# Summing the key products of a Performer block by 32x32 blocks turned on VectorE, in place of products on TensorE

## The chip, the core and the metric

One core of one Trainium2 chip runs the whole kernel in one launch. The metric is the device time in microseconds (us) from the launch's start to its end. The engines are TensorE (PE, with its weight loads PEld), VectorE (DVE), ScalarE (ACT), GpSimd (POOL) and SyncE (SP), which here issues all transfers.

## What is computed

Rows are 8 batches of 1024, model width 512, 16 heads of 32, 128 random features. The part that the change touches is the linear attention's sum over the keys:

```python
pk  = phi(k * scale, omega)                     # 128 features per head
kv  = einsum('bhsm,bhsk->bhmk', pk, v)          # 128 x 32 for each head
z   = sum(pk, axis=2)                           # 128 for each head
num = einsum('bhsm,bhmk->bhsk', pq, kv)
den = einsum('bhsm,bhm->bhs', pq, z)
out = x + layernorm(x + attn) -> FFN -> layernorm, plus a gated block on shifted rows
```

## The kernel before

Three passes follow one another, each closed by a barrier of all engines: `keys_pass`, `attend_pass`, `feed_forward_pass`. Each walks 32 groups of 256 rows, four groups to a batch. fp32 products are made of three products of rounded parts (`product`, L97), so each operand is split in a hi part (ACT) and a lo part (DVE or POOL).

Each engine runs a list of jobs written out by hand, in order: `PE_BODY`, `DVE_BODY`, `ACT_BODY`, `POOL_BODY`, `SP_BODY`. An entry is (job, number, lead): in the body of group g it works on group g + lead. Engines meet in semaphores alone. No engine goes past a job whose wait isn't met.

In `keys_pass` the jobs of one body are these. `turn_x` transposes normalised rows (PE, hi on ACT, lo on DVE). `k`, `q`, `v` are products of 12 matmuls into one of three PSUM banks, `ring`. `turn_k` transposes the keys; `proj` (L652) makes the features in four banks `feat`; `top` (L565, four reductions on DVE, then `below` L569) finds the maxima; `exp` (ACT L512) makes `e`, `hi` (ACT L519) and `pk` (DVE L575) split it. `kv` (PE L676) multiplies the features of four heads by their values, 128 x 512, into a `ring` bank, from which DVE adds it to `kv_sum` (L584, L586). POOL adds the features over the rows in `z` (L457), and in `whole` (L442) puts xT together for a store. The banks bind the order: the second `k` product of a body waits until DVE has taken `kv` number 0 out of `ring[0]`, and `turn_x` number 1 waits for DVE's lo part of number 0.

What is in `kv_sum` is laid out by (32 values x 4 heads) on partitions and (4 heads x 128 features) on columns, so only the diagonal blocks are wanted, and with the features on the columns, while the next pass needs the features on partitions. The job `fold` does this for one quarter (four heads, number c) in each body after a batch has ended: for each head one matmul against the 0/1 matrix `fold` (L695), which turns and picks, and one of `z_all` against a column of ones `fold_z` (L696), both fp32, into the bank `turn`, which `turn_x` also uses. ACT copies 128 x 136 out of it to `kv_out` (L526), and after the fourth quarter SP stores `kv_out` to `kv_d` (L410). 28 bodies have one fold; the last has four, at the end of the pass.

In `attend_pass` one transfer for each batch loads `kv_in` (L856), in the pass's head for batch 0, and as the last SP job of a batch's first group for the next. ACT and DVE split it into `kvz` (L1062 to L1163). SP's list in a body begins with `load_x` and then carries the denominators out, back, inverted out and back (`den_store`, `den_load`, `rden_store`, `rep_load`), which DVE's `recip` (L1132) waits for.

Of the kernel before, what the change touches and what calls it, by code (L numbers as in the profile page):

```python
# [242 lines left out]
def keys_pass(nc, x, wq, wk, wv, omega, xn_d, xT_d, u_d, kv_d, n_batches, groups_per_batch):  # L243
# [11 lines left out]
    with ctx:  # L255
# [51 lines left out]
        fold_made, folded, fold_out = sem("fold_made"), sem("folded"), sem("fold_out")  # L307
# [32 lines left out]
        def fold_bank(g, c):  # L340
            return feat[c].t if g == G - 1 else turn

        def rows(j):
# [3 lines left out]
        PE_BODY = [("kv", 0, -1), ("proj", 0, 0), ("k", 0, 1), ("kv", 1, -1), ("k", 1, 1), ("kv", 2, -1), ("q", 0, 1),  # L347
                   ("proj", 1, 0), ("turn_k", 0, 1), ("kv", 3, -1), ("q", 1, 1), ("turn_k", 1, 1), ("v", 0, 1),
                   ("fold", 0, -1), ("turn_x", 0, 2), ("v", 1, 1), ("turn_x", 1, 2)]
        DVE_BODY = [("top", 0, 0), ("kv", 0, -1), ("kv", 1, -1), ("stats", 0, 2), ("kv", 2, -1), ("sq", 0, 1),  # L350
                    ("top", 1, 0), ("turn_k", 0, 1), ("pk", 0, 0), ("pk", 1, 0), ("pk", 2, 0), ("kv", 3, -1),
                    ("turn_k", 1, 1), ("sq", 1, 1), ("pk", 3, 0), ("pk", 4, 0), ("pk", 5, 0), ("turn_x", 0, 2),
                    ("v_out", 0, 1), ("pk", 6, 0), ("v_out", 1, 1), ("turn_x", 1, 2), ("pk", 7, 0)]
# [13 lines left out]
        def run(eng, do, order):  # L367
            def body(g, b, i):

                for job, n, lead in order:  # L370
# [3 lines left out]
                    if job == "fold" and not pieces(g + lead) or job == "sums" and NC - 1 not in pieces(g + lead):  # L374
                        continue
# [11 lines left out]
        def _(sp):  # L387
# [3 lines left out]
            def do(job, n, g, b, i):  # L391
# [1206 lines left out]
```

## Time and profile before

| | us |
|---|---|
| median of 3 runs | 3691.76 (3691.68 to 3693.3) |
| profiled execution, time | 3692.05 |
| its span, first to last instruction | 3690.2 |
| TensorE busy | 3544.2 (96%) |
| VectorE busy | 2070.7 (56%) |
| ScalarE busy | 1839.5 (50%) |
| GpSimd busy | 1394.2 (38%) |

The keys pass lasts until about 948 us of the span, the attend pass until about 2120, the rest is the feed-forward pass. Busy shares are means over all three; the rows further below are from single bodies. L12 is line 12 of the kernel.

### The profile page before, as it was taken

To read this page: it belongs to the slowest core of one execution; us is meant where nothing else is said; L and a number is where in the kernel's file an instruction comes from. 1 tells how busy PE (TensorE), PEld (TensorE's weight loads), DVE (VectorE), ACT (ScalarE), POOL (GpSimd) and SP (SyncE) were. 2 spreads that over 40 slices of the span, in tenths; PEclk is the share of its full clock that TensorE was granted. 3 is DMA by queue.
4 is the path that set the end of the run, shared out by engine and by line. 5 is a ranking of instruction groups with operands and counts; after the bars stand their busy time and mean duration, and the time that the engine had idled before them with its cause. 6 is when DMAs were issued, how large, how long until landed. Compare 5 with 4: busy or idle time off the path is not lost. (4 is left out here: it accounts for less than half of the span.)

```text
span 3690.2 us, 71667 instructions
## 1 busy us (share of the span) xinstructions
PE 3544.2 (96%) x27762; PEld 3105.4 (84%) x27762; DVE 2070.7 (56%) x3304; ACT 1839.5 (50%) x3976; POOL 1394.2 (38%) x957
## 2 busy tenths in 40 slices
PE   7999999999699999999999949999999999999998
PEld 6888888887588888888888849988889989888887
DVE  5877777777567777777777633333333333333332
ACT  5777777777456656565665633333333323333332
POOL 2554545454244545454454412222222222222222
PEclk9999999999799999999999979999999999999999
DMA  2222222221223232232323241111111111111111
GB/s 104 87 78 70 90 78 73 73 88 54 95 81 102 82 97 91 88 97 88 102 84 98 83 129 68 46 44 43 45 44 46 45 38 46 44 43 45 45 45 46
DMA packets 151680, 262.70 MB, mean 71 GB/s; under 512 B 23184, under 2 KB 44176, under 8 KB 151440
## 3 DMA queue, kind: packets, MB, share of 16 engines
q1 hardware_dynamic: 151440, 259.46, 20.9%
q8 instruction: 155, 2.54, 0.3%
q14 instruction: 85, 0.70, 0.1%
HBM read 155.48 MB, written 103.94 MB: 70 GB/s over the span
## 5 line engine op out<-in xcount | busy, mean ns | idle before, releaser
L1484 DVE TENSOR_TENSOR ffn_hT_lo<-ffn_hid,ffn_hT_hi 128x512 fp32r<-128x512 f32 x256 | 334.3, 1334 | 489.4 <-ACT ffn_hT_hi L1460 489.4
L97 PE MATMUL ffn_hidden<-ffn_yT_hi,ffn_wa_hi 128*128 128x256 f32 x2048 | 573.3, 280 | 11.8 <-DVE ffn_yT_lo L1480 11.8
L97 PE MATMUL ffn_hidden<-ffn_yT_hi,ffn_wa_lo 128*128 128x256 f32 x2048 | 573.3, 280 | 0.0
L97 PE MATMUL ffn_hidden<-ffn_yT_lo,ffn_wa_hi 128*128 128x256 f32 x2048 | 572.3, 279 | 0.0
L1451 ACT ACTIVATE ffn_hid<-ffn_hidden,ffn_bias 128x256 f32<-128x256 f32 x512 | 213.2, 467 | 669.6 <-PE ffn_hidden L97 650.8
L233 POOL TENSOR_TENSOR ffn_n_rstd<-ffn_n_base,ffn_n_power 128x2 f32<-128x2 f32 x32 | 22.4, 700 | 1073.7 <-DVE ffn_n_negmean L228 1073.7
L97 PE MATMUL ffn_result<-ffn_wb_hi,ffn_hT_hi 128*128 128x512 f32 x1024 | 412.2, 403 | 2.6 <-DVE ffn_hT_lo L1484 2.6
L97 PE MATMUL ffn_result<-ffn_wb_hi,ffn_hT_lo 128*128 128x512 f32 x1024 | 404.5, 395 | 0.0
L97 PE MATMUL ffn_result<-ffn_wb_lo,ffn_hT_hi 128*128 128x512 f32 x1024 | 404.2, 395 | 0.0
L97 PEld LDWEIGHTS ffn_hidden<-ffn_yT_hi,ffn_wa_hi 128*128 128x128 f32 x2048 | 384.5, 188 | 20.8 <-DVE ffn_yT_lo L1480 12.1
L97 PEld LDWEIGHTS ffn_hidden<-ffn_yT_lo,ffn_wa_hi 128*128 128x128 f32 x2048 | 385.0, 188 | 8.8
L97 PEld LDWEIGHTS ffn_hidden<-ffn_yT_hi,ffn_wa_lo 128*128 128x128 f32 x2048 | 385.2, 188 | 0.0
L457 POOL TENSOR_TENSOR keys_z_sum<-keys_z_sum,keys_e 128x512 f32<-128x512 f32 x192 | 265.2, 1402 | 307.3 <-ACT keys_e L512 307.3
L512 ACT ACTIVATE keys_e<-keys_feat,keys_below 128x128 f32<-128x128 f32 x1024 | 280.6, 420 | 22.8 <-DVE keys_below L569 22.7
L575 DVE SCALAR_TENSOR_TENSOR keys_pk_lo<-keys_e,keys_pk_hi 128x512 fp32r<-128x512 f32 x256 | 219.3, 887 | 25.7 <-ACT keys_pk_hi L519 25.5
L97 PEld LDWEIGHTS ffn_result<-ffn_wb_hi,ffn_hT_hi 128*128 128x128 f32 x1024 | 192.1, 188 | 48.4 <-DVE ffn_hT_lo L1484 10.2
L97 PEld LDWEIGHTS ffn_result<-ffn_wb_hi,ffn_hT_lo 128*128 128x128 f32 x1024 | 192.2, 188 | 46.9
L1107 DVE TENSOR_REDUCE attend_top<-attend_feat 128x4 f32<-128x512 f32 x256 | 159.0, 684 | 125.3 <-PE attend_feat L1200 125.3
L1126 DVE SCALAR_TENSOR_TENSOR attend_pT_lo<-attend_feat,attend_pT_hi 128x512 fp32r<-128x512 f32 x256 | 163.3, 683 | 116.7 <-ACT attend_pT_hi L988 116.3
L97 PEld LDWEIGHTS ffn_result<-ffn_wb_lo,ffn_hT_hi 128*128 128x128 f32 x1024 | 192.4, 188 | 38.0
L565 DVE TENSOR_REDUCE keys_top<-keys_feat 128x4 f32<-128x512 f32 x256 | 159.0, 684 | 107.7 <-PE keys_feat L652 107.7
L1464 ACT ACTIVATE ffn_s<-ffn_s,ffn_n_shift,ffn_n_rstd 128x512 f32<-128x512 f32 x64 | 48.7, 809 | 338.7 <-POOL ffn_n_shift L235 338.7
(238 smaller groups left out, 9876.8 us busy)
## 6 DMA issues: line engine op xcount, KB each, us to landing
attend_uq<-u_d SPq DMA_DIRECT2D x33, 512.0 KB, 4.6
ffn_y_in<-y_d SPq DMA_DIRECT2D x33, 512.0 KB, 3.6
keys_xin<-in_L_attn_x_dram SPq DMA_DIRECT2D x32, 512.0 KB, 5.3
xn_d<-keys_xn SPq DMA_DIRECT2D x32, 512.0 KB, 4.2
xT_d<-keys_xT_whole SPq DMA_DIRECT2D x32, 512.0 KB, 2.6
u_d<-keys_uq SPq DMA_DIRECT2D x32, 512.0 KB, 2.8
attend_xTf<-xT_d SPq DMA_DIRECT2D x32, 512.0 KB, 5.1
r_d<-attend_gate SPq DMA_DIRECT2D x32, 512.0 KB, 3.2
```

The costliest lines, as they stand in the source:

```text
L97: last = pe.matmul(out, stationary[a], moving[b], start=start and n == 0, stop=stop and n == len(TERMS) - 1)
L233: pool.tensor_tensor(self.rstd[:, :], self.base[:, :], self.power[:, :], ALU.pow).then_inc(self.root, 1)
L457: pool.tensor_tensor((z_all if last_of_batch else z_sum)[:, c, :], z_sum[:, c, :], e[t][:, c, :], ALU.add).then_inc(z_added[t], 1)
L512: last = act.activation(e[t][:, c, j * M:(j + 1) * M], feat[j].t[:, c * M:(c + 1) * M], ACT.Exp, bias=below[:, t, h:h + 1])
L565: dve.tensor_reduce(top[:, n, :, j:j + 1], feat[j].t[:, :].rearrange("p (c m) -> p c m", c=NC), AX.X, ALU.max).then_inc(top_ready, 1)
L575: dve.scalar_tensor_tensor(out=pk[t].lo[:, c, :], in0=e[t][:, c, :], scalar=FLOOR, in1=f32(pk[t].hi[:, c, :]), op0=ALU.add, op1=ALU.subtract)\
L1107: dve.tensor_reduce(top[:, n, :, j:j + 1], feat[j].t[:, :].rearrange("p (c m) -> p c m", c=NC), AX.X, ALU.max).then_inc(feat[j].free, 1)
L1126: dve.scalar_tensor_tensor(out=pT[j].lo[:, :], in0=feat[j].t[:, :], scalar=FLOOR, in1=f32(pT[j].hi[:, :]), op0=ALU.add, op1=ALU.subtract)\
L1451: last = act.activation(hid[n % 2][:, a, :], bank.t[:, a * GT:(a + 1) * GT], ACT.Gelu, bias=bias1[:, 2 * n + a:2 * n + a + 1])
L1464: act.activation(s[:, t, :], s[:, t, :], ACT.Identity, bias=norm.shift[:, t:t + 1], scale=norm.rstd[:, t:t + 1]).then_inc(normed, 1)
L1484: dve.tensor_tensor(hT[n % HB].lo[:, :, :], hid[n % 2][:, :, :], f32(hT[n % HB].hi[:, :, :]), ALU.subtract).then_inc(h_ready[n % HB], 1)
```

## The change

The products of `fold` go. In `keys_pass` the job `fold` is now DVE's: for one quarter it turns `kv_sum[:, c, :]` by 32x32 blocks into `kv_turned`, turns `z_all[:, c, :]` into `z_turned`, and reduces the latter by blocks of 32 into `z_part`. SP stores `kv_turned` (256 KB) after each quarter and `z_part` after the fourth. The constants `fold` and `fold_z`, ACT's copy, and the wait of `turn_x` on it are gone. The load in `attend_pass` becomes 20 transfers for a batch: 16 gather the diagonal blocks of `kv_d` in runs of 32 numbers into `kv_parts`, which has two halves of each sum, and 4 bring `z_parts`. A new DVE job `fold` there adds the two halves and the four parts of z into `kv_in`. All five orders of the keys pass are rewritten, and DVE's of the attend pass has one job more.

```diff
         PE_BODY = [("kv", 0, -1), ("proj", 0, 0), ("k", 0, 1), ("kv", 1, -1), ("k", 1, 1), ("q", 0, 1), ("kv", 2, -1),
                    ("proj", 1, 0), ("turn_k", 0, 1), ("kv", 3, -1), ("q", 1, 1), ("turn_k", 1, 1), ("v", 0, 1),
                    ("turn_x", 0, 2), ("v", 1, 1), ("turn_x", 1, 2)]
+        DVE_BODY = [("top", 0, 0), ("kv", 0, -1), ("kv", 1, -1), ("stats", 0, 2), ("sq", 0, 1), ("kv", 2, -1),
+                    ("top", 1, 0), ("turn_k", 0, 1), ("sq", 1, 1), ("pk", 0, 0), ("pk", 1, 0), ("kv", 3, -1),
+                    ("pk", 2, 0), ("turn_k", 1, 1), ("pk", 3, 0), ("pk", 4, 0), ("fold", 0, -1), ("turn_x", 0, 2),
+                    ("pk", 5, 0), ("pk", 6, 0), ("v_out", 0, 1), ("v_out", 1, 1), ("turn_x", 1, 2), ("pk", 7, 0)]
+        ACT_BODY = [("k", 0, 1), ("exp", 0, 0), ("exp", 1, 0), ("exp", 2, 0), ("exp", 3, 0), ("k", 1, 1),
+                    ("hi", 0, 0), ("hi", 1, 0), ("hi", 2, 0), ("q", 0, 1), ("norm", 0, 2), ("turn_k", 0, 1),
+                    ("hi", 3, 0), ("exp", 4, 0), ("exp", 5, 0), ("turn_k", 1, 1), ("hi", 4, 0), ("q", 1, 1),
+                    ("hi", 5, 0), ("exp", 6, 0), ("turn_x", 0, 2), ("hi", 6, 0), ("v_out", 0, 1), ("exp", 7, 0),
+                    ("v_out", 1, 1), ("turn_x", 1, 2), ("hi", 7, 0)]
+        POOL_BODY = [("z", 0, 0), ("z", 1, 0), ("z", 2, 0), ("z", 3, 0), ("stats", 0, 2), ("whole", 0, 1),
                      ("z", 4, 0), ("z", 5, 0), ("z", 6, 0), ("z", 7, 0)]
-        SP_BODY = [("x", 0, 2), ("whole", 0, 1), ("sums", 0, -1), ("q", 1, 1), ("norm", 0, 2)]
+        SP_BODY = [("x", 0, 2), ("norm", 0, 2), ("q", 1, 1), ("sums", 0, -1), ("whole", 0, 1)]
...
+                    for m, c in enumerate(pieces(g)):
+                        wait_alone(sp, fold_out, pieces_before(g) + m + 1, sp_passed)
+                        sp.dma_start(kv_d[b][:, c, :], turned_to(g, c)).then_inc(sums_stored, 16)
+                        if c == NC - 1:
+                            sp.dma_start(z_d[b], z_part[:, :, :, :].rearrange("p m c j -> p (m c j)")).then_inc(sums_stored, 16)
...
-                        act.activation(kv_out[:, c * HC:(c + 1) * HC, :],
-                                       fold_bank(g, c)[:, 0:HC * KW].rearrange("p (h k) -> p h k", k=KW), ACT.Copy)\
-                            .then_inc(fold_out, 1)
...
+                    for c in pieces(g):
+                        dve.wait_ge(kv_added, NC * last_group + c + 1)
+                        dve.wait_ge(z_added[1], NC * last_group + c + 1)
+                        if g == G - 1:
+                            dve.wait_ge(pk_ready[0], NC * G)
+                        wait(dve, sums_stored, stored_before(b, 0 if g == G - 1 else c))
+                        dve.transpose(turned_to(g, c), kv_sum[b % 2][:, c, :]).then_inc(kv_ready, 1)
+                        wait(dve, fold_out, NC * b + c)
+                        dve.transpose(z_turned[:, :], z_all[:, c, :]).then_inc(z_blocks, 1)
+                        dve.wait_ge(z_blocks, NC * b + c + 1)
+                        dve.tensor_reduce(z_part[:, :, c, :].rearrange("p m j -> p j m"),
+                                          z_turned[:, :].rearrange("p (j m q) -> p j m q", j=HC, m=NC), AX.X, ALU.add)\
+                            .then_inc(fold_out, 1)
...
-                        for j in range(HC):
-                            out = fold_bank(g, c)[:, j * KW:j * KW + M]
-                            pe.matmul(out, kv_sum[b % 2][:, c, j * M:(j + 1) * M], fold[:, j % 2, :], start=True, stop=False)
-                            last = pe.matmul(out, z_all[:, c, j * M:(j + 1) * M], fold_z[:, :], start=False, stop=True)
-                        last.then_inc(folded, 1)
...
-            sp.dma_start(kv_in[:, :, :, :].rearrange("p c j k -> p (c j k)"), kv_d[b]).then_inc(kv_loaded, 16)
+            own = kv_d[b].rearrange("p c (i a m k) -> p c i a m k", i=2, a=2, m=NC)
+            for m in range(NC):
+                to = slice(m * KD, (m + 1) * KD)
+                for a in range(2):
+                    for s in range(2):
+                        at = (2 * a + s) * KD
+                        sp.dma_start(kv_parts[to, :, a::2, s, :], own[at:at + KD, :, :, a, m, :]).then_inc(kv_loaded, 16)
+                sp.dma_start(z_parts[to, :, :], z_d[b].rearrange("(t r) (m h) -> r t m h", t=NC, m=NC)[:, :, m, :])\
+                    .then_inc(kv_loaded, 16)
...
+        DVE_BODY = [("top", 0, 0), ("top", 1, 0), ("fold", 0, 0), ("recip", 0, -1), ("below", 0, 0), ("mix", 0, 1),
...
+                    dve.tensor_tensor(kv_in[:, :, :, 0:KD], kv_parts[:, :, :, 0, :], kv_parts[:, :, :, 1, :], ALU.add)
+                    dve.tensor_reduce(kv_in[:, :, :, KD:KD + 1], z_parts[:, :, :].rearrange("p t (c j) -> p c j t", c=NC), AX.X,
+                                      ALU.add).then_inc(kv_folded, 1)
```

## Rows read from the trace of the kernel before

**Rows 1.** Busy time in two bodies of the keys pass, without and with a fold.
```profile
core 0: us, PE busy (x) PEld busy (x) DVE busy (x) ACT busy (x) POOL busy (x), PEclk, DMA share, GB/s
130.33:156.50 26.17, 25.85 (x218) 21.57 (x217) 21.33 (x37) 20.29 (x54) 14.58 (x11) 1.00 0.23 82
212.94:241.15 28.21, 27.70 (x234) 23.49 (x233) 21.31 (x36) 20.46 (x55) 14.68 (x11) 1.00 0.22 76
```

**Rows 2.** Timeline of PE around one fold; start, length, engine, line, what, idle before.
```profile
398.06 0.39 PE L97 MATMUL keys_ring<-keys_wv_hi,keys_xT_lo 128*128 128x512 f32 x1
398.49 0.49 PE L695 MATMUL keys_turn<-keys_fold,keys_kv_sum 128*128 128x128 f32 x2
...
401.01 0.63 PE L608 MATMUL keys_turn<-keys_ident,keys_xn 128*128 128x128 f32 x4 [0.47 <-ACT keys_kv_out L526]
```

**Rows 3.** Timeline of DVE in a body with a fold, from one `top` to the next.
```profile
419.19 2.48 DVE L565 TENSOR_REDUCE keys_top<-keys_feat 128x4 f32<-128x512 f32 x4 [2.97 <-PE keys_feat L652]
429.63 0.69 DVE L575 SCALAR_TENSOR_TENSOR keys_pk_lo<-keys_e,keys_pk_hi 128x512 fp32r<-128x512 f32 x1 [0.64 <-ACT keys_pk_hi L519]
433.27 0.69 DVE L550 TENSOR_TENSOR keys_v_parts<-keys_ring,keys_v_parts 128x512 fp32r<-128x512 f32 x1 [0.75 <-ACT keys_v_parts L496]
435.51 2.48 DVE L565 TENSOR_REDUCE keys_top<-keys_feat 128x4 f32<-128x512 f32 x4 [0.35 <-PE keys_feat L652]
```

**Rows 4.** Timeline of DVE in a body without a fold.
```profile
139.63 2.48 DVE L565 TENSOR_REDUCE keys_top<-keys_feat 128x4 f32<-128x512 f32 x4 [2.97 <-PE keys_feat L652]
142.92 2.98 DVE L575 SCALAR_TENSOR_TENSOR keys_pk_lo<-keys_e,keys_pk_hi 128x512 fp32r<-128x512 f32 x3
147.02 0.67 DVE L559 TENSOR_REDUCE keys_sq<-keys_squares 128x16 f32<-128x512 f32 x1
147.62 2.45 DVE L575 SCALAR_TENSOR_TENSOR keys_pk_lo<-keys_e,keys_pk_hi 128x512 fp32r<-128x512 f32 x3
153.91 1.29 DVE L565 TENSOR_REDUCE keys_top<-keys_feat 128x4 f32<-128x512 f32 x2
```

**Rows 5.** Timelines of PE and DVE: what binds a `top` to the next.
```profile
410.02 0.69 DVE L584 COPY keys_kv_sum<-keys_ring 128x512 f32<-128x512 f32 x1
411.01 0.40 PE L97 MATMUL keys_ring<-keys_wk_hi,keys_xT_hi 128*128 128x512 f32 x1
```

**Rows 6.** Timelines of POOL and DVE: splits with the sums beside them, and without.
```profile
423.27 4.57 POOL L457 TENSOR_TENSOR keys_z_sum<-keys_z_sum,keys_e 128x512 f32<-128x512 f32 x3 [4.56 <-ACT keys_e L512]
478.91 1.89 DVE L575 SCALAR_TENSOR_TENSOR keys_pk_lo<-keys_e,keys_pk_hi 128x512 fp32r<-128x512 f32 x3
```

**Rows 7.** Timelines of DVE, ACT and SP at the end of the keys pass.
```profile
938.52 0.69 DVE L586 TENSOR_TENSOR keys_kv_sum<-keys_ring,keys_kv_sum 128x512 f32<-128x512 f32 x1 [0.26 <-PE keys_ring L676]
945.66 0.28 ACT L526 ACTIVATE keys_kv_out<-keys_feat 128x136 f32<-128x136 f32 x1 [1.50 <-PE keys_feat L696]
```

**Rows 8.** Timelines of SP, DVE and PE in the head of the attend pass.
```profile
949.80 1.86 SPq L863 DMA_DIRECT2D attend_squares<-in_L_attn_omega_dram  x4
954.75 0.47 SPq L856 DMA_DIRECT2D attend_kv_in<-kv_d  x1
956.94 0.53 SPq L874 DMA_DIRECT2D attend_mu<-in_L_ffn_mu_r_dram  x1
964.26 1.67 DVE L1094 SCALAR_TENSOR_TENSOR attend_mixed<-attend_diff,attend_mu,attend_xTf 128x256 f32<-128x256 f32 x4 [1.19 <-DMA attend_mu<-in_L_ffn_mu_r_dram]
```

**Rows 9.** Transfers from 949.5 to 952.9 us: packets under 512 B, and their share of 16 engines.
```profile
q1 hardware_dynamic: 576, 0.07, 12.8%
```

**Rows 10.** Timelines of SP and POOL around a load of `kv_in` inside the attend pass.
```profile
1157.33 0.82 SPq L856 DMA_DIRECT2D attend_kv_in<-kv_d  x1
1158.26 0.58 SPq L885 DMA_DIRECT2D attend_xTf<-xT_d  x1
1167.05 1.30 SPq L893 DMA_DIRECT2D den_d<-attend_raw  x2
1131.05 1.90 POOL L949 TENSOR_TENSOR attend_diff<-attend_xTf 128x1024 f32<-128x1024 f32 x1
```

**Rows 11.** Timelines of DVE and PE in the body of the attend pass before that.
```profile
1136.30 0.34 DVE L1132 RECIPROCAL attend_rden<-attend_den 128x32 f32<-128x32 f32 x1
1137.01 0.29 DVE L1121 TENSOR_TENSOR attend_below_parts<-attend_below,attend_below_parts 128x128 fp32r<-128x128 f32 x1
1139.58 0.38 PE L1209 MATMUL attend_turn<-attend_ident,attend_below_parts 128*128 128x128 f32 x2
```

More of the change, by code:

```diff
@@ L338, in pieces_before, with turned_to, stored_before @@
             return max(0, g - GB + 1)
-        def fold_bank(g, c):
-            return feat[c].t if g == G - 1 else turn
+        def turned_to(g, c):
+            return e[0][:, c, :] if g == G - 1 else kv_turned[:, :]
+        def stored_before(b, c):
+            return 16 * ((NC + 1) * b + c)
         def rows(j):
             return slice(j * KD, (j + 1) * KD)
-        PE_BODY = [("kv", 0, -1), ("proj", 0, 0), ("k", 0, 1), ("kv", 1, -1), ("k", 1, 1), ("kv", 2, -1), ("q", 0, 1),
+        PE_BODY = [("kv", 0, -1), ("proj", 0, 0), ("k", 0, 1), ("kv", 1, -1), ("k", 1, 1), ("q", 0, 1), ("kv", 2, -1),
@@ L348, in keys_pass @@
                    ("proj", 1, 0), ("turn_k", 0, 1), ("kv", 3, -1), ("q", 1, 1), ("turn_k", 1, 1), ("v", 0, 1),
[L349 to L353, printed above, removed]
@@ L373, in body @@
                     own_b, own_i = (i + lead) // GB, (i + lead) % GB
-                    if job == "fold" and not pieces(g + lead) or job == "sums" and NC - 1 not in pieces(g + lead):
+                    if job in ("fold", "sums") and not pieces(g + lead):
                         continue
@@ L602, in do @@
                         wait(pe, k_split, 2 * g)
-                        wait(pe, fold_out, pieces_before(g - 2))
                     else:
@@ L819, in attend_pass @@
                    ("num", 2, 0)]
-        DVE_BODY = [("top", 0, 0), ("top", 1, 0), ("recip", 0, -1), ("below", 0, 0), ("mix", 0, 1), ("kv", 0, 0),
-                    ("exp", 0, 0), ("o", 0, -1), ("out", 0, 0), ("sq", 0, 1), ("turn_q", 0, 1), ("sq", 1, 1),
-                    ("out", 1, 0), ("mix", 1, 1), ("hi", 1, 0), ("turn_q", 1, 1), ("wo", 0, -1), ("wo", 1, -1),
-                    ("stats", 0, -1)]
+        DVE_BODY = [("top", 0, 0), ("top", 1, 0), ("fold", 0, 0), ("recip", 0, -1), ("below", 0, 0), ("mix", 0, 1),
+                    ("kv", 0, 0), ("exp", 0, 0), ("o", 0, -1), ("out", 0, 0), ("sq", 0, 1), ("turn_q", 0, 1),
+                    ("sq", 1, 1), ("out", 1, 0), ("mix", 1, 1), ("hi", 1, 0), ("turn_q", 1, 1), ("wo", 0, -1),
+                    ("wo", 1, -1), ("stats", 0, -1)]
         ACT_BODY = [("num", 3, -1), ("norm", 0, -2), ("k", 0, 0), ("k", 1, 0), ("below", 0, 0), ("kv", 0, 0),
@@ L835, in attend_pass @@
                 ("sq", 1), ("weights", 7)]
-        OF_BATCH = ("kv",)
+        OF_BATCH = ("kv", "fold")
+        KV_LOADS = 5 * NC
         def run(eng, do, order):
```

77 lines of the change are left out of this document (25 added, 52 removed).

## The prediction

> **What bounds the kernel now.** I read the busy time by stretch first, then the timelines of PE and DVE over single bodies, because the change touches the keys pass and a mean over the span says nothing of it. In a keys body with a fold PE is busy 27.70 of 28.21 us at full granted clock, in one without 25.85 of 26.17 [rows 1]. So at first sight a fold costs PE's time and nothing else. But DVE is the second thing to look at. Without a fold, from `top` number 1 at 139.63 to the next `top` at 153.91, DVE works 14.28 us without a gap [rows 4]; with a fold the same stretch takes 16.32 us (419.19 to 435.51), of which 2.0 are idle in waits on ACT and 0.35 on PE [rows 3] (two of the three or four ACT waits are shown, 0.64 and 0.75; two of 0.31 make up the rest). So bodies without a fold are already set by PE and DVE together, and in the others PE's fold gives DVE its only slack. That is what the change spends.
>
> **What goes.** From the last matmul of `v` at 398.06 the next would start 0.23 later, at 398.29; with the fold `turn_x` starts at 401.01 [rows 2]. A fold thus holds PE for 2.72 us, its wait for ACT's copy included. There are 28 in steady bodies: 76 us if nothing but PE counted, which would make a body 25.5 us. The bodies without a fold, 26.17 [rows 1], show that at most 2.04 of the 2.72 come free even when DVE gets no new work: 28 times 2.04 is 57 us. ACT's copy (0.28 each [rows 7]) is off the path.
>
> **What comes on DVE.** Two turns of 128x512 and one reduction of 128x512. The reduction has a row of the same size: 0.67 long, 0.60 from start to start [rows 4]. A turn has no row. Its lower bound is that pitch, 0.60, as every 128x512 pass of DVE in rows 3 to 5 has it; its upper bound is two such passes, 1.2, if 4-byte numbers need two. I take 0.60, since copy, sum and reduction all have it. The reduction waits for the turn before it, so one overlap of 0.08 is lost. Fold: 1.95 us, bounds 1.9 to 3.15.
>
> **The loop that sets a body.** DVE's `top` 0, then `below` and the evacuation of `kv` 0, which ends 3.4 us after `top` started; then PE's second `k` may begin. In the body shown the evacuation ends at 410.71 and that product starts at 411.01, so 0.25 of slack is left there [rows 5]. From the start of that product to `top` 1 is 8.18 (411.01 to 419.19 [rows 3, 5]): `k`, `q`, `kv` and `proj` on PE, whose sum the swap of `q` and `kv` leaves as it is. Stretch A from `top` 0 to `top` 1 is 3.46 + 8.18 = 11.64 us, in which DVE idles 4 us that the new order does not fill either. Stretch B, back to `top` 0, is DVE's own work. Without contention it is 2.68 for `top` and `below` and 16 passes of 0.60, 12.3 us; measured are 14.28, so 2.0 are contention: three splits in a row take 2.98 with POOL's sums beside them and 1.89 without [rows 4, 6]. The splits read two SBUF operands; the new passes read one. The Trainium skill, page "SBUF — State Buffer", section "Who interferes with whom", says the same: a VectorE instruction with at most one SBUF input outside the 2-port modes does not contend with GpSimd. By that rule the fold takes no contention of its own; if the rule were wrong here, each turn could wait for one POOL sum, 1.3 us.
>
> In the new order `pk` 0 to 3 alternate with other passes and meet `z` 4 to 6 (1.3 to 1.6 us each [rows 6]) one by one: by hand 1.1 + 0.5 + 0.9 = 2.5 of contention; `z` 7 falls beside the fold and costs nothing. Where the sums wait for the fold (one body in four) they meet `pk` 5 to 7 instead, about 2.2. Between the 2.0 of today and 2.5 I take 2.3, as the alternation can't be read off. A body with a fold: 11.64 + 12.3 + 1.95 + 2.3 = 28.2 us, bounds 26.9 (contention 1.0, since fewer splits stand in a row) and 29.4 (fold 3.15). Today: 28.21. **27 such bodies: 0, bounds -35 and +32 us.** PE's 2.72 us turn into waits: `turn_x` 0 for the late `turn_k` 1, `turn_x` 1 for the late `turn_x` 0, `k` 1 for `kv` 0. Bodies 1 to 3 without a fold: 26.2 to 26.5 each, +1 in all.
>
> SP now has `sums` ahead of `whole` and of the next `x`, and waits there for the fold on DVE. Who is queued: the xT store and the x load, some 5 us later than today. x is read by `stats` in stretch A, where DVE idles 4 us; this hides it.
>
> **End of the keys pass.** Today from the last sum on DVE (938.52, ends 939.21) to the end of ACT's last copy is 6.7 us [rows 7], with PE folding beside DVE. Now four folds in a row follow the last sum: 4 x 2.0 = 8.0, then two stores instead of one, +0.4. The fold in body 31 delays `pk` 5 to 7, on which PE waits there: +1.5. Sum: **+3.5 us**, bounds +1 and +9.
>
> **Head of the attend pass.** 20 issues take the place of one. Four issues of 128 runs of 128 B take 1.86, or 0.47 each; that of `kv_in` takes 0.47 [rows 8]. 20 x 0.49 - 0.5 = +9.3 us ahead of the constants `gain`, `offset` and `mu`, and DVE's first mix waits for `mu` (964.26 [rows 8]). Since the landing of `mu` is 7.3 us after its issue at 956.94, behind 2.6 MB of weights that are through by then, some 3 to 4 of the 9.3 are taken up. **+6 us**, bounds +3 and +12. The small packets themselves: 576 of them take 12.8% of 3.4 us on 16 engines [rows 9], 0.012 engine-us each, so 4608 take 3.5 us, less than their issue. The skill's page "DMA: Bandwidth & Descriptors", section "Specifications", wants 512 B or more in a transfer's pieces for full rate; this speaks against the 128 B runs, yet by the row they stay hidden behind the issue. By a full doubling of the row's price the head would be 3.5 us later.
>
> **Inside the attend pass.** The 20 issues come before `load_x` and `den_store` once a batch. Today: `kv_in` issued at 1157.33, `load_x` at 1158.26, `den_store` at 1167.05 [rows 10]. New: `load_x` near 1167.1, landed near 1172; POOL's difference is due 36.7 us (a body) after 1131.05 [rows 10], 1167.8, and is 4 us late; `mix` on DVE comes after `recip` and `below`, six us later, and takes it. `den_store` is late by 0.7, and `recip` had 1.7 of slack. DVE's new `fold`, 0.7 + 0.2, stands before `recip`; `below_parts` end at 1137.30, PE wants them at 1139.58 [rows 11]: 2.3 of slack. **0 us**, bounds 0 and +30.
>
> **Sum** against the profiled execution's 3692.05 (median 3691.76, so 0.3 apart, nothing): 0 + 1 + 3.5 + 6 + 0 = +10.5, **3703 us**, 0.3% slower. A comparison of this kernel can tell about 0.2%, 7.4 us, from no change.
>
> **Rivals.** (1) *PE stays the bound.* If the new order let DVE's work fall into the 4 us of stretch A or removed all contention, a body would be 26.2 us: 28 x 2.04 = -57, +10.5, so 3645. For it: PE's 96% [rows 1]. Against it: 14.28 us of gapless DVE work already without a fold [rows 4]. 8%. (2) *Contention falls.* The alternation saves 1.1 us of it per body: -30 + 10.5, 3672. 15%. (3) *A turn costs two passes*, or waits for POOL: fold 3.15, +32 + 3 + 10.5, 3738. It decides from 0.9 us a turn on. 13%. (4) *The issues block the attend pass.* `kv_in` took 0.82 us to issue within the pass [rows 10]. At 0.8 each, 20 are 16 us; `den_store` is 7 us late, less 1.7 and 2.3 of slack is 3 us of PE stall in each of 8 batches, and the head is 6 worse: +30, 3733. It decides from 0.55 us an issue on. 14%. (5) *TensorE loses its clock* in the new gaps. The granted clock is 1.00 with today's small gaps [rows 1]; 3%, 3800 or more. The forecast, its band 3690 to 3715: 47%.
>
> **Chances and range.** Below 3684.4 lie rivals 1 and 2: 0.22 with a little of the forecast's lower side. Within 0.2%, to 3699.1: 0.27, the lower half of the forecast's band. Above: 0.51. The range leaves out rival 1 and the far parts of 2, 3 and 5: 3672 to 3738. The forecast's own: 3690 to 3715.
>
> **What the profile after would show.** Turns near 0.68 us long and 0.60 apart on DVE. Bodies of about 28.2 us in which PE is busy near 25.3 and waits on DVE: before `turn_x` (L608) and before the second `k`. DVE without idle time from `top` 1 to `top` 0. `mu` and the first mix near 6 us later in the head. Wrong would be: PE without waits in the keys pass (rival 1), splits in a row at 0.6 (rival 2), a turn of 1 us or more (rival 3), an idle PE in the attend pass before `below` (rival 4).

## The result, and the profile after

The changed kernel takes 3771.36 us (median of 4 runs, 3767.57 to 3772.46), the kernel before 3691.72 (3685.24 to 3693.3). The ratio is 1.022, its 95% interval [1.020, 1.024]: 2.2% slower, where 0.3% slower was forecast. The profiled execution of after spans 3769.2 us against 3690.2, so 79.0 us are to be found.

The page of after, its first part:

```profile
PE 3510.7 (93%) x27250; PEld 3066.0 (81%) x27250; DVE 2213.1 (59%) x3416; ACT 1839.7 (49%) x3944; POOL 1380.8 (37%) x952
```

This says only that PE is still the busiest engine. Where the time went shows once the span is cut at instructions that both kernels have: DVE's first instruction of the attend pass, its first and its last `top` there. Timelines of DVE, after; start, length, engine, line, what, count, and in brackets the idle time before it and what ended it; the second fence groups all of the line, with its first and last start:

```profile
966.54 0.06 DVE L1063 MEMSET attend_xTf<- 128x4 f32 x1 [4.48 <-PEq L54]
1011.66 2.47 DVE L1100 TENSOR_REDUCE attend_top<-attend_feat 128x4 f32<-128x512 f32 x4
```
```profile
L1100 DVE TENSOR_REDUCE attend_top<-attend_feat x256: 677/683/694, 1011.7 to 2183.5; 128x4 f32<-128x512 f32 x128
```

And the same of before:

```profile
949.88 0.06 DVE L1070 MEMSET attend_xTf<- 128x4 f32 x1 [10.68 <-PEq L54]
983.76 2.47 DVE L1107 TENSOR_REDUCE attend_top<-attend_feat 128x4 f32<-128x512 f32 x4
```
```profile
L1107 DVE TENSOR_REDUCE attend_top<-attend_feat x256: 674/682/694, 983.8 to 2104.6; 128x4 f32<-128x512 f32 x128
```

| stretch | before | after | difference | forecast |
|---|---|---|---|---|
| keys pass, to DVE's first instruction of attend | 949.9 | 966.5 | +16.7 | +4.5 |
| head of attend, to the first `top` | 33.9 | 45.1 | +11.2 | +6 |
| inside attend, first to last `top` | 1120.8 | 1171.8 | +51.0 | 0 |
| the rest | | | +0.1 | 0 |

Two thirds of the loss lie inside the attend pass, which the forecast put at nothing.

**The keys pass.** Busy time by stretch in a body without a fold and in one with it, the counterpart of [rows 1]:

```profile
core 0: us, PE busy (x) PEld busy (x) DVE busy (x) ACT busy (x) POOL busy (x), PEclk, DMA share, GB/s
140.05:166.88 26.83, 25.60 (x217) 21.77 (x218) 21.63 (x37) 20.35 (x55) 12.93 (x12) 1.00 0.23 80
397.62:426.28 28.66, 26.00 (x217) 21.75 (x218) 23.98 (x40) 20.57 (x55) 13.05 (x12) 1.00 0.24 84
```

PE now works 26.00 of 28.66 us where it worked 27.70 of 28.21: its fold is gone and the time is not. The timeline of DVE in that second body, from `top` 1 to the next `top` 0:

```profile
396.14 0.69 DVE L571 TENSOR_TENSOR keys_kv_sum<-keys_ring,keys_kv_sum 128x512 f32<-128x512 f32 x1 [3.35 <-PE keys_ring L676]
397.62 2.48 DVE L550 TENSOR_REDUCE keys_top<-keys_feat 128x4 f32<-128x512 f32 x4 [0.79 <-PE keys_feat L652]
401.49 2.38 DVE L560 SCALAR_TENSOR_TENSOR keys_pk_lo<-keys_e,keys_pk_hi 128x512 fp32r<-128x512 f32 x2
...
406.10 2.34 DVE L560 SCALAR_TENSOR_TENSOR keys_pk_lo<-keys_e,keys_pk_hi 128x512 fp32r<-128x512 f32 x2
408.37 0.70 DVE L582 STREAM_TRANSPOSE keys_kv_turned<-keys_kv_sum 128x512 f32<-128x512 f32 x1
409.00 0.66 DVE L584 STREAM_TRANSPOSE keys_z_turned<-keys_z_all 128x512 f32<-128x512 f32 x1
409.69 0.69 DVE L586 TENSOR_REDUCE keys_z_part<-keys_z_turned 128x16 f32<-128x512 f32 x1
414.55 1.88 DVE L550 TENSOR_REDUCE keys_top<-keys_feat 128x4 f32<-128x512 f32 x3
```

After `top` 1 no idle time is given until 414.55: stretch B is 16.93 us of work, the fold in it 1.93 (408.37 to the next pass at 410.30). Ahead of `top` 1, in stretch A, DVE idles 3.35 and 0.79 us. So work was put into the full stretch with an empty one beside it.

**The attend pass.** SP's timeline at a change of batch, after (before, one issue stood here, [rows 10]):

```profile
1040.56 2.52 SPq L847 DMA_DIRECT2D attend_kv_parts<-kv_d  x4
1043.12 0.60 SPq L848 DMA_DIRECT2D attend_z_parts<-z_d  x1
...
1053.40 0.60 SPq L848 DMA_DIRECT2D attend_z_parts<-z_d  x1
1054.12 0.55 SPq L878 DMA_DIRECT2D attend_xTf<-xT_d  x1
1054.79 1.46 SPq L886 DMA_DIRECT2D den_d<-attend_raw  x2
```

From 1040.56 to 1054.12 are 13.56 us for 20 issues, 0.68 each. What hangs on them, on POOL, on DVE and on PE:

```profile
1059.50 1.90 POOL L942 TENSOR_TENSOR attend_diff<-attend_xTf 128x1024 f32<-128x1024 f32 x1 [13.85 <-DMA attend_xTf<-xT_d]
1061.35 2.49 POOL L950 TENSOR_TENSOR attend_ka_lo<-attend_act_k,attend_ka_hi 128x512 fp32r<-128x512 f32 x2
```
```profile
1060.00 0.35 DVE L1125 RECIPROCAL attend_rden<-attend_den 128x32 f32<-128x32 f32 x1 [2.34 <-DMA attend_den<-den_d]
1060.27 1.18 DVE L1106 SCALAR_TENSOR_TENSOR attend_below<-attend_sq,attend_top 128x32 f32<-128x32 f32 x1
1061.48 1.23 DVE L1112 CAST attend_below_parts<-attend_below 128x128 fp32r<-128x128 f32 x1
1062.74 1.25 DVE L1114 TENSOR_TENSOR attend_below_parts<-attend_below,attend_below_parts 128x128 fp32r<-128x128 f32 x1
```
```profile
1064.05 0.44 PE L1208 MATMUL attend_turn<-attend_ident,attend_below_parts 128*128 128x128 f32 x2 [3.03 <-DVE attend_below_parts L1114]
```

Three things follow one another. `recip` waits 2.34 us for `den`, which is stored late. POOL's difference, which waits 13.85 us for its data (2.01 at the same change in the kernel before), now runs beside DVE's three small operations, and these take 1.18, 1.23 and 1.25 us; in the kernel before they took 0.15, 0.23 and 0.29 (1029.84 to 1030.57). PE waits 3.03 us for them, and the stretch behind it runs in part at 1.2 GHz, the lower of TensorE's two levels. This is the first change of batch; at the third PE waits 4.09 us, and the 4 us behind that wait are all at the lower level (second row):

```profile
1064.05:1068.05 4.00, 4.00 (x41) 3.46 (x42) 1.52 (x4) 2.40 (x6) 0.00 (x0) 0.57 0.62 192
1362.82:1366.82 4.00, 4.00 (x40) 3.35 (x41) 4.00 (x3) 2.14 (x5) 3.84 (x4) 0.50 0.29 97
```

A granted clock of 0.57 over 4.00 us costs 1.7 us, the least of the eight batches; in the others 8 us behind the wait have 0.50 in the first half and 0.73 to 0.90 in the second, and the mean of all eight is 2.6 us. Over the pass, the lines that write the wait down (engine, line, what was waited for, us in total, times) are, for L1208:

```profile
  DVE attend_below_parts L1114: 68.9, 16
```

PE and its weight loads are counted apart here; PE's own eight waits are 32.7 us of it, 4.1 a batch. With the clock's 2.6 that is 6.7 a batch, an estimate of 53 us beside the 51.0 measured, so the two account for the whole. The wait has two parts. From the start of `recip` to the end of the third small operation are 0.99 us in the kernel before and 2.96 to 3.99 in the eight batches of after: 21 of the 32.7 us are the long operations, the rest is `recip` itself coming late.

In the head the same 20 issues stand ahead of the constants:

```profile
971.12 2.75 SPq L847 DMA_DIRECT2D attend_kv_parts<-kv_d  x4
...
985.28 0.43 SPq L867 DMA_DIRECT2D attend_gain<-in_L_attn_ln_g_dram  x1
```
```profile
992.04 1.67 DVE L1087 SCALAR_TENSOR_TENSOR attend_mixed<-attend_diff,attend_mu,attend_xTf 128x256 f32<-128x256 f32 x4 [12.57 <-DMA attend_mu<-in_L_ffn_mu_r_dram]
```

14.2 us of issues, and the first `mix` waits 12.57 us for `mu` where it waited 1.19 [rows 8].

### The profile page after: what moved, and what is told of

It reads as the page before. It is cut to its first block and busy times, and to the rows that moved or that the text cites. A ratio compares the mean times of both kernels' runs of the same rounds, so it can differ in the third digit from the quotient of the medians.

```text
span 3769.2 us, 70946 instructions
## 1 busy us (share of the span) xinstructions
PE 3510.7 (93%) x27250; PEld 3066.0 (81%) x27250; DVE 2213.1 (59%) x3416; ACT 1839.7 (49%) x3944; POOL 1380.8 (37%) x952
## 5 line engine op out<-in xcount | busy, mean ns | idle before, releaser
L560 DVE SCALAR_TENSOR_TENSOR keys_pk_lo<-keys_e,keys_pk_hi 128x512 fp32r<-128x512 f32 x256 | 250.2, 1008 | 0.0
L1488 DVE SCALAR_TENSOR_TENSOR ffn_x_in<-ffn_r_in,ffn_x_in 128x1024 f32<-128x1024 f32 x32 | 39.2, 1225 | 295.6 <-DMA ffn_r_in<-r_d 295.6
```

Source lines behind the costliest of these rows:

```text
L560: dve.scalar_tensor_tensor(out=pk[t].lo[:, c, :], in0=e[t][:, c, :], scalar=FLOOR, in1=f32(pk[t].hi[:, c, :]), op0=ALU.add, op1=ALU.subtract)\
L1488: dve.scalar_tensor_tensor(out=x_in[:, :, :], in0=r_in[:, :, :], scalar=0.5, in1=x_in[:, :, :], op0=ALU.mult, op1=ALU.add).then_inc(base_r ...
```

## The experiments

The theory: the attend pass loses to SP's time for the issues and to what they delay, the keys pass to the fold's place in DVE's full stretch. The rivals: the traffic of small pieces, DVE's new work in the attend pass, contention with GpSimd, the new orders. The kernel before was timed beside them on the same chip (3690.6, 3690.2 and 3688.7 us in the three sessions, 3691.7 with the result above), so a difference between runs of two sessions can be off by some 3 us.

**The issues moved.** The same transfers, issued where SP is idle.

```diff
-                   ("rep_load", 0, -1), ("store_y", 0, -2), ("xb", 0, -1), ("store_r", 0, 0), ("sq", 1, 1),
-                   ("kv", 0, 0)]
+                   ("rep_load", 0, -1), ("store_y", 0, -2), ("xb", 0, -1), ("kv", 0, 0), ("store_r", 0, 0),
+                   ("sq", 1, 1)]
```

> The kernel after, with SP's 20 loads of the next batch's sums issued behind the load of xb and ahead of the store of r, not as the last job of the body; the same transfers, the same packets, the same bytes. Theory 1 (issue time): the attend pass lost 51 us because 13.6 us of issues stand ahead of load_x, den_store and den_load; behind xb SP is idle for some 10 us in every body, so 40 to 50 us come back: 3771 - 45 = 3726 (3720 to 3732). In the trace a body behind a batch change takes 35.2 to 36 us again, and the wait of recip for den is gone. Theory 2 (traffic): the 128 and 64 byte pieces, or the new work on VectorE, are what costs; then the time is moved, not saved, and the kernel stays within 10 us of 3771.

Measured: 3719.24 us (3716.2 to 3720.58), 52 less than after. The small operations of DVE behind `recip`, at the same change of batch:

```profile
1055.29 0.35 DVE L1125 RECIPROCAL attend_rden<-attend_den 128x32 f32<-128x32 f32 x1 [0.37 <-DMA attend_den<-den_d]
...
1055.72 0.23 DVE L1112 CAST attend_below_parts<-attend_below 128x128 fp32r<-128x128 f32 x1
```

The wait is 0.37 in the place of 2.34, the operations are short again, and the stretch from first to last `top` is back at 1120.9 us (1009.1 to 2130.0). Packets, bytes and DVE's sum and reduction are all still there. So the 51 us were a matter of place on SP's queue; traffic and new work cost nothing that shows (1120.9 us against 1120.8 before).

**The issues alone, three doses.** The kernel before, with further loads that nothing reads behind its own load of `kv_in` in the body.

```diff
                     load_kv(sp, after(b, n_batches))
+                    load_more(sp, b)
...
+            own = kv_d[b].rearrange("p (c j k) -> p c j k", c=NC, j=HC)
+            for m in range(NC):
+                to = slice(m * KD, (m + 1) * KD)
+                for a in range(2):
+                    for s in range(2):
+                        at = (2 * a + s) * KD
+                        sp.dma_start(kv_parts[to, :, a::2, s, :], own[at:at + KD, :, a::2, 0:KD]).then_inc(more_loaded, 16)
+                if m < NC - 1:
+                    sp.dma_start(z_parts[to, :, :], kv_d[b][:, 0:H].rearrange("(t r) h -> r t h", t=NC))\
+                        .then_inc(more_loaded, 16)
```

For 14 and 9 loads the loop over `m` ends sooner.

> The kernel before, with 19 further loads behind its own load of kv_in in the body (the shapes of the kernel after: 16 of 256 pieces of 128 bytes, 3 of 128 pieces of 64 bytes; nothing reads them), in each of the 8 batches; the head of the attend pass and the keys pass are left as they are. It measures the issues alone, without the fold on VectorE. Theory 1 (issue time): 3691.7 + 8 x 5.5 = 3736 (3730 to 3743), nearly all of the 51 us inside the attend pass. Theory 2a (the new work on VectorE, its sum and its reduction ahead of recip, is what delays the chain): no more than 10 us above the kernel before, 3702.

> The kernel before with 14 further loads in the body (12 of 256 pieces of 128 bytes, 2 of 128 pieces of 64 bytes). 9 of them cost nothing, 19 cost 51 us (6.4 us a batch, for some 12.2 us of issues). Theory 1 (slack of about 6 us, then one to one): 9.0 us of issues cost 3 us a batch, 3691 + 25 = 3716 (3709 to 3723). Theory 2 (more slack, and then a step, since TensorE's wait also takes its clock): under 3 us, or the whole 51.

> The kernel before with 9 further loads in the body (8 of 256 pieces of 128 bytes, 1 of 128 pieces of 64 bytes) in the place of 19, so 5.7 us of issues in each batch where 19 have 12.2. Theory 1 (slack in the chain of den up to some 4 to 7 us, beyond it each us of issues costs one): 12.2 us cost 6.4 a batch, so 5.7 us cost 0 to 1, in all 3692 to 3700. Theory 2 (every issue costs, as queue or packet time does): half of 51, 3716.

| further loads | issues, first batch | time | against before |
|---|---|---|---|
| 9 | 7.3 us | 3689.9 | 1.000 [0.999, 1.001] |
| 14 | 9.5 us | 3696.1 | 1.002 [1.001, 1.003] |
| 19 | 13.3 us | 3741.9 | 1.014 [1.012, 1.016] |

One of the ten executions with 9 loads took 11448.5 us; nothing on record says why, and it does not move the median. 19 loads alone cost 51 us, the whole of the loss inside the attend pass. But the price is neither linear nor a plain threshold: 9 are free, 14 cost 6 to 7 us in all, and the last 5, 3.8 us of issues a batch, cost some 45 us, 5.6 a batch. The timelines of DVE say why. With 14 (first) and with 19 (second), same change of batch:

```profile
1029.56 0.23 DVE L1135 CAST attend_below_parts<-attend_below 128x128 fp32r<-128x128 f32 x1
```
```profile
1032.62 1.22 DVE L1135 CAST attend_below_parts<-attend_below 128x128 fp32r<-128x128 f32 x1
```

With 14 loads POOL's late difference lengthens one of DVE's three small operations at most changes of batch, two at one of them (0.76 and 1.39 us), and never the cast; with 19 it lengthens all three at every change. PE waits 35.2 us for them in all with 19 loads and 1.6 with 14. The first theory's 3716 for 14 loads was 20 us too high, the second's step is what was seen.

**The head.** The loads of batch 0 behind all weights, not ahead of the constants.

```diff
             load_w(sp, range(2, 3))
-            load_kv(sp, 0)
...
             load_w(sp, range(3, len(halves_of)))
+            load_kv(sp, 0)
```

> The kernel after, with the 20 loads of the first batch in the head of the attend pass issued behind all loads of constants and weights, not ahead of gain, offset and mu. Theory 1: the first mix on VectorE no longer waits 12.6 us for mu, so the head's 11.2 us come back: 3771 - 11 = 3760 (3757 to 3763). Theory 2 (what costs is elsewhere, as weights that arrive late behind the 2.3 to 2.5 MB in the queues): the mix is followed by the next wait for weights, and under 4 us come back.

Measured: 3765.78 us (3763.71 to 3770.41), 5.6 less, half of what was expected. The head itself gave back 10.5 us (967.81 to 1002.41, 34.6), but the stretch from first to last `top` became 4.5 longer: in the first body POOL's difference now waits 12.0 us, since `load_x` of the next group is queued behind the 20 issues. Nearly half of the gain was handed on to the next job of the queue.

**The fold in DVE's idle time.** Only the last four folds, which must follow the last sum, stay behind `pk` 4.

```diff
-        DVE_BODY = [("top", 0, 0), ("kv", 0, -1), ("kv", 1, -1), ("stats", 0, 2), ("sq", 0, 1), ("kv", 2, -1),
+        DVE_BODY = [("top", 0, 0), ("kv", 0, -1), ("kv", 1, -1), ("stats", 0, 2), ("sq", 0, 1), ("fold", 0, -1), ("kv", 2, -1),
...
-                    ("pk", 2, 0), ("turn_k", 1, 1), ("pk", 3, 0), ("pk", 4, 0), ("fold", 0, -1), ("turn_x", 0, 2),
+                    ("pk", 2, 0), ("turn_k", 1, 1), ("pk", 3, 0), ("pk", 4, 0), ("fold", 1, -1), ("turn_x", 0, 2),
...
-                if job == "fold":
+                if job == "fold" and n == (g == G - 1):
```

> The kernel after, with the fold of the bodies 4 to 31 placed on VectorE ahead of the sum of kv 2, where VectorE idles 3.35 us in each body, and not behind pk 4; only the last four folds stay where they are. Theory 1 (VectorE's own work from the second top to the next first top sets the keys body, 11.7 + 16.9 us, and the fold is 1.93 of it): a body falls from 28.66 to 26.8, near that of the bodies without a fold (26.84): 27 x 1.85 = 50, so 3721 (3715 to 3732). Theory 2 (the body is set by something else, as TensorE's chain behind kv 2 or the contention with GpSimd): the fold delays kv 2 and so the bank that the second k or the projection waits for, and the time changes by less than 10 us.

Measured: 3726.29 us (3724.93 to 3729.78), 45 less. Timelines of POOL and DVE, and the busy time of a body:

```profile
403.81 5.06 POOL L451 TENSOR_TENSOR keys_z_sum<-keys_z_sum,keys_e 128x512 f32<-128x512 f32 x4 [6.44 <-ACT keys_e L506]
```
```profile
405.70 0.70 DVE L582 STREAM_TRANSPOSE keys_kv_turned<-keys_kv_sum 128x512 f32<-128x512 f32 x1
406.33 0.66 DVE L584 STREAM_TRANSPOSE keys_z_turned<-keys_z_all 128x512 f32<-128x512 f32 x1
407.03 0.69 DVE L586 TENSOR_REDUCE keys_z_part<-keys_z_turned 128x16 f32<-128x512 f32 x1
408.94 0.69 DVE L569 COPY keys_kv_sum<-keys_ring 128x512 f32<-128x512 f32 x1 [1.23 <-PE keys_ring L676]
```
```profile
437.64:464.49 26.85, 25.62 (x217) 21.79 (x218) 23.75 (x40) 20.36 (x55) 14.20 (x12) 1.00 0.26 89
```

DVE still idles 1.23 us behind the fold, and the body takes 26.85 us, as after's bodies without a fold (26.83): the fold is free there. And it lies wholly beside POOL's four sums (403.81 to 408.87), while in after both turns ran with POOL idle (its sums there ended at 407.30 and began again at 409.82); the lengths are the same, 0.70 and 0.66, so a turn does not contend. The Trainium skill, page "SBUF — State Buffer", section "Who interferes with whom", has the rule that an instruction with one SBUF input outside the 2-port modes does not contend with GpSimd. The section does not name the turn; these rows behave as the rule says.

**What the contention costs.** POOL adds only 32 of 512 columns of `z` 4 to 7; the other columns of these sums are left out, and `z_all` is set to one at the start.

```diff
+                        w_ = slice(0, HC * M if t == 0 else 32)
-                        pool.tensor_tensor((z_all if last_of_batch else z_sum)[:, c, :], z_sum[:, c, :], e[t][:, c, :],
+                        pool.tensor_tensor((z_all if last_of_batch else z_sum)[:, c, w_], z_sum[:, c, w_], e[t][:, c, w_],
```

> The kernel after, in which GpSimd adds only 32 of the 512 columns of each of the sums z 4 to 7 (the other columns of the denominators' sums are left out, and z_all is set to one for them); VectorE's work is unchanged. Theory 1 (2.7 us of each keys body is VectorE waiting for the SBUF port shared with GpSimd): the splits of pk take 0.6 from start to start, a body with a fold falls from 28.66 to some 26.2, where TensorE's chain sets it, and the time is 3771 - 27 x 2.4 - 2 = 3704 (3695 to 3720). Theory 2 (the splits are slow for another reason, as their two operands or a wait): under 10 us.

Measured: 3694.54 us (3690.73 to 3699.49), 77 less. The splits of this kernel, grouped over 300 to 880 us (count | busy, mean ns | idle), the busy time of a body, and the splits of after:

```profile
L563 DVE SCALAR_TENSOR_TENSOR keys_pk_lo<-keys_e,keys_pk_hi 128x512 fp32r<-128x512 f32 x180 | 119.2, 693 | 0.0
```
```profile
396.83:422.88 26.05, 25.84 (x217) 21.83 (x218) 21.34 (x40) 20.41 (x55) 10.03 (x12) 1.00 0.26 92
```
```profile
L560 DVE SCALAR_TENSOR_TENSOR keys_pk_lo<-keys_e,keys_pk_hi 128x512 fp32r<-128x512 f32 x160 | 156.9, 1010 | 0.0
```

A split falls from 1010 to 693 ns, a body from 28.66 to 26.05: with 8 splits a body that is 2.5 us of contention, and 2.6 are gained. It is paid in full in stretch B, which falls from 16.93 to 14.33, while stretch A stays at 11.72.

**The old orders.** All orders of the keys pass as before (DVE's is shown), the fold behind `pk` 5.

```diff
+        DVE_BODY = [("top", 0, 0), ("kv", 0, -1), ("kv", 1, -1), ("stats", 0, 2), ("kv", 2, -1), ("sq", 0, 1),
+                    ("top", 1, 0), ("turn_k", 0, 1), ("pk", 0, 0), ("pk", 1, 0), ("pk", 2, 0), ("kv", 3, -1),
+                    ("turn_k", 1, 1), ("sq", 1, 1), ("pk", 3, 0), ("pk", 4, 0), ("pk", 5, 0), ("fold", 0, -1), ("turn_x", 0, 2),
+                    ("v_out", 0, 1), ("pk", 6, 0), ("v_out", 1, 1), ("turn_x", 1, 2), ("pk", 7, 0)]
```

> The kernel after, with the orders of all engines in the keys pass as in the kernel before and the fold on VectorE put in behind pk 5 (three splits in a row, z 0 behind whole on GpSimd). It separates the new orders from the moved work. Theory 1 (alternating the splits with other passes costs 0.7 us of contention more a body: 26.84 against 26.17 in the bodies without a fold): 30 x 0.65 = 20 less, 3751 (3745 to 3760). Theory 2 (the new orders are what the work on VectorE needs, or make no difference): 3765 or more.

Measured: 3774.87 us (3770.41 to 3776.8), no gain. Two bodies that follow one another, 4 us of the second, and the wait of PE ahead of these:

```profile
421.06:449.16 28.10, 25.85 (x217) 21.57 (x218) 22.87 (x40) 20.32 (x56) 14.58 (x11) 1.00 0.25 86
449.16:480.33 31.17, 28.93 (x217) 24.12 (x218) 22.99 (x40) 20.26 (x55) 14.54 (x11) 0.89 0.22 77
464.00:468.00 4.00, 4.00 (x52) 3.59 (x53) 2.49 (x5) 0.09 (x1) 2.73 (x1) 0.50 0.96 311
```
```profile
462.26 0.63 PE L608 MATMUL keys_turn<-keys_ident,keys_xn 128*128 128x128 f32 x4 [2.10 <-DVE keys_xT_lo L531]
```

The splits are cheaper here, 872 ns against 1010 in the same stretch of time, which is 1.1 us a body where the first theory said 0.7, and most bodies take 28.1. But PE waits 2.1 us in one piece, where in the new orders it waits 1.23 and 1.19 in two (434.99 and 439.55 in after), and behind some of these waits its clock falls to 1.2 GHz: of the 20 bodies from 339 to 923 us six take 31.2 and two 29.6. The body before, with a wait of 2.11, kept its clock, so the length of the wait alone does not settle it. The second theory was right in its number; the lower contention is real, and the bodies at the lower clock take it back.

**One more pass.** A second turn of `z_all` into a buffer that nothing reads.

```diff
+                        dve.transpose(z_again[:, :], z_all[:, c, :])
                         dve.transpose(z_turned[:, :], z_all[:, c, :]).then_inc(z_blocks, 1)
```

> The kernel after, with a second turn of the same 128x512 of z_all into a buffer that nothing reads, so four passes a fold in the place of three. Theory 1 (VectorE's work sets the body, one to one; a turn costs 0.62 from start to start): 31 x 0.62 = 19 more, 3790 (3786 to 3796). Theory 2 (a turn has a hidden price behind it, or TensorE's waits grow into a lower clock): over 3800. Theory 3 (TensorE sets the body): under 3776.

Measured: 3779.88 us (3777.41 to 3785.75), 8.5 more, or 11.5 when each is taken against the kernel before of its own session, and not 19; all three theories missed. The mean of 20 bodies is 29.16 us, 0.42 over after's, which is 11 us in 27. DVE does set the body, but not one to one: the pass stands where the splits behind it met POOL's last sum. In most bodies `pk` 5 and 6 take 1.28 us together (at 439.05) where they take 1.58 in after (at 439.32), and stretch B grows by 0.27; in the bodies that end a batch it grows by 0.6, nearly the whole pass.

**All three places.** The fold in the idle time, the loads of the body behind `xb`, and the head's loads in two halves, each where SP waits for a free stage.

```diff
-            load_w(sp, range(3, len(halves_of)))
+            load_w(sp, range(3, 5))
+            load_kv(sp, 0, range(0, 2))
+            load_w(sp, range(5, len(halves_of)))
+            load_kv(sp, 0, range(2, NC))
```

> The kernel after with all three places put right: the fold of the bodies 4 to 31 in VectorE's idle time, the 20 loads of the body behind the load of xb, and the loads of the head in two halves, ten behind the loads of gate and xb and ten behind the last weights, where SP waits for free stages anyway. Theory 1 (the three losses are of different places and add up: 52 inside the attend pass, 45 in the keys pass, up to 10 in the head): 3771 - 52 - 45 - 9 = 3665 (3658 to 3675), 0.7% faster than the kernel before. Theory 2 (they share a cause, or what one gives the other takes): above 3690.

Measured: 3664.28 us (3660.21 to 3666.01), ratio to before 0.993 [0.992, 0.995]. The losses add up as they were taken apart; the head is 35.0 us (918.37 to 953.35), 1.1 over before.

**All three, in the old orders.**

> The kernel all_three (fold in VectorE's idle time, loads behind xb, head in halves), with the orders of the keys pass of the kernel before on all engines. Bodies with the fold behind pk 5 took 28.1 us in these orders where TensorE kept its clock and 31.2 where its granted clock fell after a wait of 2.1 us at turn_x. Theory 1 (in the old orders the contention with GpSimd is 2.0 instead of 2.7 us a body, and with the fold out of the way TensorE no longer waits 2 us at turn_x, so its clock stays): bodies of 26.2 to 26.5 against 27.0, 3664 - 28 x 0.65 = 3646 (3638 to 3655). Theory 2 (the clock still falls in these orders): 3664 or more.

Measured: 3642.19 us (3641.26 to 3643.38), ratio to before 0.988 [0.986, 0.989], the fastest of all. A body with a fold, busy time and DVE's timeline:

```profile
428.31:454.48 26.17, 25.85 (x217) 21.56 (x218) 23.23 (x40) 20.32 (x56) 14.60 (x11) 1.00 0.27 91
```
```profile
426.58 0.69 DVE L586 TENSOR_REDUCE keys_z_part<-keys_z_turned 128x16 f32<-128x512 f32 x1
428.31 2.49 DVE L550 TENSOR_REDUCE keys_top<-keys_feat 128x4 f32<-128x512 f32 x4 [1.03 <-PE keys_feat L652]
```

26.17 us is to the hundredth the body without a fold of [rows 1], with PE busy 25.85 of it and its clock whole. So with the fold in stretch A the old orders are the better ones, by 22 us; they only could not bear the fold in stretch B.

## Why the prediction was wrong

**Bodies of the keys pass.** The mechanism was right, and so were its terms: stretch A 11.64 (measured 11.73), a turn near 0.68 long (0.70 and 0.66), the fold 1.95 (1.93), no contention of the fold's own. One term was mis-sized: contention in stretch B, taken as 2.3 between 2.0 and 2.5, measured as 16.93 - 12.3 - 1.93 = 2.7. With stretch A's 0.1 this makes 28.66 in the place of 28.2. The bodies' mean was 28.74:

```profile
169.46 0.17 DVE L554 SCALAR_TENSOR_TENSOR keys_below<-keys_sq,keys_top 128x16 f32<-128x16 f32 x1
...
916.58 0.17 DVE L554 SCALAR_TENSOR_TENSOR keys_below<-keys_sq,keys_top 128x16 f32<-128x16 f32 x1
```

(747.12 us in 26 bodies of after.) Against 28.21 [rows 1] that is +14, and the three bodies without a fold, 26.83 against the 26.2 to 26.5 foreseen, add 2. The working had counted 2.5 and then took less "as the alternation can't be read off"; the 2.5 was the nearer, and 27 bodies multiply each tenth by 27. The sum also treated contention as a constant of the order; the further turn shows that it moves with a shift (0.3 us in most bodies).

**End of the keys pass.** Forecast +3.5, measured +16.7 - 15.6 = +1.1 (the last `top` came 15.6 us later, at 939.46 against 923.89). The terms as written, 8.0 - 6.7 + 0.4 + 1.5, add up to 3.2 and not 3.5. The four folds took 7.7 us as said, and from their end to DVE's first instruction of attend are 4.5 us, where 3.9 followed ACT's last copy. What did not come is the 1.5 for the late `pk` 5 to 7: body 31's fold (945.76) stands behind the last `top`, and yet the last sum ended 14.9 us after that `top`, 0.4 sooner than before (15.3). Why it cost nothing there stays open.

**Head.** Forecast +6 with bounds of +3 and +12, measured +11.2. The price of an issue failed: 14.2 us for 20 is 0.71 each, not 0.49, and of the slack of 3 to 4 us between `mu` and the mix 2.6 were there (13.7 us more of issues, the mix 11.1 later from the pass's start). The rows it went by were of loads of 128 pieces; 16 of the 20 have 256.

**Inside the attend pass.** This is the step that failed, 0 against +51.0, beyond its upper bound of 30. It went by 0.49 us an issue, which kept `load_x` 9.8 us behind the first issue and made `den_store` 0.7 late. At 0.68 each `load_x` came 13.5 us behind it, and in the second batch `den_store` was 4.5 late (14.2 us behind the first issue, 9.7 before), past the 1.7 us of slack that `recip` was given. It was rival 4 that came about, given 14% and 3733 for the whole. Its price of 0.8 was too high, but its point was right: 0.68 us an issue, past the 0.55 from which it was to decide; DVE's own fold, as said, cost nothing (the issues alone give the same 51). Two things were missing from it. The working followed `load_x` and `den_store` each on its own: `load_x` 4 us late "is taken", because `mix` stands behind `recip` and `below`. It asked what the late difference delays, but not what it now runs beside: POOL's two operations fall upon three of DVE's small ones, and 0.7 us of work become 3.7. That eats the 2.3 us of slack that the sum relied on. And PE's wait of some 4 us also takes its clock, 2.6 us more on the mean. Per batch 6.4 us were measured where the rival had 3.

**The rivals.** Rival 1, PE as the bound with 3645 us, was turned down because DVE's work in stretch B has no gap. That was right for the change as made. Yet the 57 us it spoke of are there to be had: with the fold in stretch A and the issues out of the way 3642 were measured. The working had itself noted "DVE idles 4 us that the new order does not fill". Rival 2, less contention by alternation, had the wrong sign: alternating the splits costs more, 1010 against 872 ns a split in the two orders, and in bodies without a fold stretch B is 15.00 us in after against the 14.28 of [rows 4]. Rival 3, a turn of two passes, fell with the turns' 0.70 and 0.66 us. Rival 5, the clock, was given 3%; in the new orders the keys pass keeps it (0.99 from 120 to 900 us), in the attend pass it is lost for a few us a batch, and in the old orders in eight bodies of twenty.

**The range** reached to 3738, the price of one rival at a time. Nothing kept a rival and the misses of the other terms from coming together, and two small misses (+12 in the keys pass, +5 in the head) of the same sign as the large one (+51) made 68 us above the forecast.

## What to carry to other kernels

A fold of three passes is cheap or dear by its place alone: put work that needs nothing at once into the stretch where its engine already waits, here 45 us better than the same work 16 us later in the body. When one transfer becomes twenty, the first price is the issuing queue's time, 0.68 to 0.81 us each here; look for the longest idle stretch of that queue, and ask of each job behind them not only what it delays but which engine's work its own users will then run beside. A cost with slack ahead of it is best measured in doses: 9 loads showed nothing, 14 next to nothing, 19 the whole 51 us.

## What was not expected of the hardware

- A turn of 128x512 fp32 in blocks of 32x32 takes 0.70 or 0.66 us, 0.59 to 0.63 from start to start, about as any other pass of DVE of that size, and is not lengthened beside GpSimd's sums.
- An issue of a load of 256 pieces of 128 B, or of 128 of 64 B, holds SP for 0.60 to 0.64 us, at times more (3.90 for four, 0.99 for one), against mostly 0.43 to 0.47 (at times 0.82) for one of 128 long rows. The landing took 2.2 and 2.0 us. The pieces' rate was no limit inside the pass, with 5441 packets of the queue in the 16 us around one batch's 20 loads (from 1040 to 1056 us in after):

```profile
q1 hardware_dynamic: 5441, 1.48, 42.3%
```

- Small operations suffer the most from contention for their size: 128x128 on DVE went from 0.23 and 0.29 us to 1.23 and 1.25 beside a GpSimd operation of about that length, the cast among them although it reads one tensor. The Trainium skill, page "SBUF — State Buffer", section "Who interferes with whom", says that casts can enter the 2-port modes, which do contend, and that operations with two SBUF inputs contend with a GpSimd instruction that reads SBUF; the rows agree with both, though none shows which mode the cast ran in.
- Behind waits of the same length, 2.10 and 2.11 us, TensorE's granted clock fell once and stayed once. What decides it stays open here; the new orders, with two waits of 1.2 us, went with a clock of 0.99 instead of 0.96 from 120 to 900 us, but they differ in more than that, so the split is not shown as the reason.
